# A two-layer graph kernel on one core: in the layer-1 visit stage SyncE runs 4000 empty loop turns ahead of the stage's closing barrier

## What is computed

```python
h = (x @ W).reshape(n, NHEAD, OUT_FEATS)                  # NHEAD 4, OUT_FEATS 64
h_l, h_r = (a_l * h).sum(-1), (a_r * h).sum(-1)
e = h_l[row] + h_r[col]
e = jnp.where(e > 0, e, ALPHA * e)
m = jax.ops.segment_max(e, row, num_segments=n)
ex = jnp.exp(e - m[row])
denom = jax.ops.segment_sum(ex, row, num_segments=n)
msg = (ex / (denom[row] + 1e-16))[:, :, None] * h[col]
out = jax.ops.segment_sum(msg, row, num_segments=n)
```

```python
xn = ln(x)
x = x + L0_gnn(xn, src, dst, edge_weight) + L0_mix(xn)
x = x + L0_ffn(ln(x))
xn = ln(x)
x = x + L1_gnn(xn, src, dst) + L1_mix(xn)
x = x + L1_ffn(ln(x))
```

## Time and profile before

| | |
|---|---|
| time, median of 3 runs | 4206.16 us (4198.36 to 4212.7) |
| span of the profiled execution | 4207.4 us |
| PE, PEld busy | 2730.2 us (65%), 2053.4 us (49%) |
| DVE busy | 2571.9 us (61%) |
| POOL busy | 2199.0 us (52%) |
| ACT busy | 1421.0 us (34%) |
| HBM traffic | 314.12 MB read, 62.05 MB written |

### The profile page before, as it was taken

The page is one execution under the profiler, slowest core; times in us unless marked ns, Lnnn a source line. Parts: engine busy times, 40 slices in busy tenths (PEclk is TensorE's granted clock), DMA queues, the critical chain, the costliest instruction groups (busy, mean ns, idle before and its releaser), DMA issues. The chain is left out here.

```text
span 4207.4 us, 47856 instructions
## 1 busy us (share of the span) xinstructions
PE 2730.2 (65%) x12850; PEld 2053.4 (49%) x12850; DVE 2571.9 (61%) x5963; ACT 1421.0 (34%) x4306; POOL 2199.0 (52%) x2162
## 2 busy tenths in 40 slices
PE   5476777577777653815666666666666655699984
PEld 4243444355555543614544444444444435599972
DVE  5346998677777786435455565556555567544438
ACT  6663000077777731113221111111111113333334
POOL 0466777666666602573256665666665641255530
PEclk9778887788989865957777777777777775699985
DMA  5332333233333223622223333333333354222234
GB/s 145 87 87 82 89 88 87 86 87 93 89 93 95 86 67 87 159 62 66 69 78 86 91 87 85 87 89 89 89 87 86 87 79 159 76 72 70 71 92 145
DMA packets 204009, 379.38 MB, mean 90 GB/s; under 512 B 48926, under 2 KB 131873, under 8 KB 203619
## 3 DMA queue, kind: packets, MB, share of 16 engines
q0 software_dynamic: 102192, 279.12, 24.7%
q1 hardware_dynamic: 101556, 97.19, 7.5%
HBM read 314.12 MB, written 62.05 MB: 89 GB/s over the span
## 5 line engine op out<-in xcount | busy, mean ns | idle before, releaser
L534 POOL DMA_INDIRECT arena<-h_table,arena x1712 | 1729.3, 1010 | 1082.5 <-issue 479.2
L548 DVE TENSOR_TENSOR arena<-arena,ps 128x260 f32 (+1 forms) x1712 | 719.3, 420 | 848.1 <-remote 355.2
L2196 PE MATMUL ps<-arena 128*128 128x260 f32 x1760 | 674.2, 527 | 376.2 <-DVE arena L548 162.2
L1216 PE MATMUL ps<-arena 128*128 128x256 f32 x1664 | 556.6, 451 | 243.4 <-DVE arena L548 133.3
L2196 PEld LDWEIGHTS ps<-arena 128*128 128x128 f32 x1760 | 411.7, 258 | 534.5 <-issue 249.7
L1216 PEld LDWEIGHTS ps<-arena 128*128 128x128 f32 x1664 | 326.6, 221 | 400.1 <-issue 237.5
L717 ACT ACTIVATE arena<-arena 128x112 f16<-128x112 f16 x1568 | 446.7, 375 | 94.5 <-DVE arena L983 77.9
L2045 ACT ACTIVATE ps<-arena 128x32 f32<-128x32 f32 x110 | 22.1, 201 | 1036.9 <-DVE arena L2109 909.5
L884 DVE TENSOR_SCALAR arena<-arena 128x128 f32<-128x128 f32 x832 | 289.5, 349 | 0.4
L2120 DVE TENSOR_TENSOR arena<-arena,ps 128x1024 f32<-128x1024 f32 x220 | 267.1, 1214 | 2.1 <-ACT ps L2045 2.1
L2570 ACT ACTIVATE arena<-ps,arena 128x128 f32<-128x128 f32 x456 | 143.6, 366 | 307.1 <-PE ps L2618 274.6
(11 more groups left out here) (525 smaller groups left out, 4486.5 us busy)
## 6 DMA issues: line engine op xcount, KB each, us to landing
arena<-h_table,arena POOLq DMA_INDIRECT x1712
arena<-in_L_ffn_w SPq DMA_DIRECT2D x32, 512.0 KB, 7.7
xn_table<-arena SPq DMA_DIRECT2D x14, 896.0 KB, 4.0
slot_out<-arena SPq DMA_DIRECT2D x21, 512.0 KB
arena<-y_rows SPq DMA_DIRECT2D x12, 896.0 KB, 9.5
h_table<-arena SPq DMA_DIRECT2D x7, 924.0 KB
h_table<-arena SPq DMA_DIRECT2D x7, 896.0 KB, 4.2
arena<-in_x SPq DMA_DIRECT2D x48, 128.0 KB
```

What stands on the lines that cost most here:

```text
L534: pool.indirect_dma_start(slot[:, 0:width], None, table, bass.IndirectOffsetOnAxis(ap=idx, axis=0)).then_inc(done, 16)
L548: dve.tensor_tensor(to, to, bank(b, width), ALU.add).then_inc(gnn_add, 1)
L1216: pe.matmul(bank(n % V0_BANKS, D), hot_w[:, g % 2, u, :], rows[:, n % RING, :], start=True, stop=True).then_inc(gnn_ps, 1)
L2196: pe.matmul(bank(4 + (g * U + u) % GNN1_BANKS, ACC_W), hot[:, b, u, :], rows[r][:, u, 0:ACC_W], start=True, stop=True).then_inc(gnn_ps, 1)
```

## The change

SP gets a function in the block of the layer-1 visits: a loop of 4000 turns with nothing in it. Nothing is taken away, and no other engine's function is touched. The loop issues no DMA and touches no semaphore; when it is through, SP goes to the block's closing barrier as before.

```diff
@@ -2011,6 +2011,7 @@
         LW = PARTS * 2 * GH
         ZERO_W = 100
+        TURNS = 4000
         assert BUCKETS * ACC_W % ZERO_W == 0
...
@@ -2018,6 +2019,11 @@
         with nc.Block() as block:
+            @block.sync
+            def _(sp):
+                with sp.Fori(0, TURNS):
+                    pass
+
             @block.gpsimd
             def _(pool):
```

## The result

The changed kernel takes 4518.18 us (median of 4 runs, 4509.96 to 4527.73) against 4203.15 us of before beside it (4 runs, 4198.36 to 4212.7): a ratio over the runs of 1.0739, 95% interval 1.0712 to 1.0766 (the two medians alone give 1.075). That is 315 us slower where 4206 us, no change, was forecast.

The account below looks back on a forecast made before the run. The visits on the other four engines, VectorE last at the barrier, were taken to bound the stage; SP's 960 us loop would hide within its 1414.4 us wait. Terms summed to 0, so 4206 us, range 4193 to 4235.

Parts of the forecast that it names:

- What bounds the kernel now: Visits stage: SP waits 1414.4 us at the closing barrier, VectorE comes last, no engine is full.
- the ring: Visits: GpSimd's gathers wait 269.1 us for TensorE, VectorE's additions 211.2 us for TensorE; SP has no part.
- The turn: SP's loop: branch 0.15 plus addition 0.09 makes 0.24 us, bounds 0.15 and 0.40, from neighbouring instructions.
- Does a running SP slow the others?: Visits: the loop adds no DMA, semaphore update or instruction fetch traffic, so it costs the other engines nothing.
- I price contention at nothing: Visits: a running SP's effect on the others put at zero, at most the scatter of the times of before.
- The sum: 4000 x 0.24 = 960 us of loop, SP at the barrier at 3007 us, 454 before VectorE; total change 0.
- The break-even of 0.354 us a turn: Closing barrier: the loop stays hidden while a turn takes less than 1414.2 / 4000 us.
- Rival A: Turn above 0.354 us makes SP last at the barrier; 4232 us at 0.36, 4392 at 0.40; chance 0.10.
- Rival B: Loop straddles an instruction-page step, each turn paying 0.34 us extra: 0.58 us a turn, 5112 us; chance 0.08.
- pushes code across the step: Loop shifts an instruction-page step of 0.34 us from behind the first load to before SP's barrier; gain put at nothing.
- Rival C: Loop isn't executed (4206 us, SP's drain stays at 2047.0), or a gain without known mechanism; first half within the 0.80.
- The range: Whole kernel: 4193 (scatter) to 4235 us (turn of 0.36 us), leaving out most of A, and B, some 0.17.

Follow-up runs that it names:

- turns_2000: Changed kernel with 2000 loop turns instead of 4000: 3658.8 us against 3658.98 of before, ratio 1.0001.
- no_gathers_2: Changed kernel, 4000 turns, GpSimd's gathers from the 33rd visit on replaced by semaphore increments; a repeat: 3747.07 us against 4211.93 of before.
- plain_dma_2: Changed kernel, 4000 turns, indirect gathers from the 33rd visit on replaced by plain DMAs of 128 rows; a repeat: 3729.37 us against 4186.04 of before.
- turns_8000: Changed kernel with 8000 loop turns instead of 4000: 4330.4 us, 671 more than before.
- nops_2: Changed kernel with 4000 written-out no-operations on SP in place of the loop; a repeat: 4219.7 us against 4211.93 of before.
- in_experts_2: Kernel before plus 1500 empty SP turns in the layer-1 expert stage, none among the visits; a repeat: 4177.47 us against 4186.04 of before.
- in_experts: Kernel before plus 1500 empty SP turns in the layer-1 expert stage, none among the visits; first run: 3659.04 us against 3670.7 of before.
- act_turns: Kernel before, no SP loop, 150 empty turns on ScalarE early in the visits; first run: 3660.87 us against 3658.98 of before.

## Why the prediction was wrong

**What bounds the kernel now** held: SP is no part of the ring, and with 2000 turns nothing moved. Of the gathers it said only that GpSimd and TensorE wait for each other. The 283.8 us of "remote" in the earlier trace rows, the largest wait of the group, were passed over. They are VectorE's wait for TensorE's counter `gnn_ps`, whose increments come late. In every trace of the long condition with all its gathers line 548 has such waits, in turns_2000, no_gathers_2 and plain_dma_2 it has none in this stage: a sign of the condition, though not yet of a held SP.

**The turn**, 0.15 + 0.09 = 0.24 us, was right for a turn that nothing disturbs: 0.225 us, 6% less. Its rows were SP's own instructions at the ends of blocks, where no gather is in flight: GpSimd's drains ahead of them are over at 1785.6 and 1978.1 us. That price was used for a stretch in which 880 gathers run. But no row of before shows the hold. Among the visits VectorE's 880 register instructions of line 548 took 69 ns each, part of the earlier trace rows, and TensorE's 880 of line 2177 took 55 ns each. So the trace could not have given the held price; the text could only have named the case. The upper bound of 0.40 us came from an instruction of VectorE and was meant for another kind of instruction, not for company; the mean, 0.430 us, is beyond it all the same.

**"Does a running SP slow the others?"** is the step that failed. Its answer, nothing, is not refuted by the runs: 1404.8 us for the others' work, and 1407.5 us with 2000 turns, but 1420 and 1422 us in two other runs with a loop. The question in the other direction, whether the others slow a running SP, was not put. "I price contention at nothing" was thus applied to both, and it left out 4000 x (0.430 - 0.225) = 820 us. With it the sum is 900 + 820 = 1720 us, against 1404.8 us of cover: 315 us, as measured. The seven tenths of cover that the forecast used up (960 of 1414 us) left room for a turn 1.5 times as dear, and it was 1.8 times.

**The sum** fails with it: SP's drain at 3779.3 instead of 3007. The break-even of 0.354 us a turn and the rule behind it (each us beyond the stage is a us of the kernel) are what the trace shows, and what turns_8000 gives at its own price.

**Rival A** has the right outcome for another reason. By its test (drain last, turn below 0.5 us, queue 14 unchanged) it is A. But its reason was a dear jump, and nops_2 shows the same holds without one. Its chance of 0.10 was drawn for that reason alone.

**Rival B** falls. Queue 14 carries the same 148 packets and 1.21 MB, and the turn is an even 0.225 us as soon as the gathers are over. That the loop pushes code across the step agrees with the trace; the first loads behind the barrier, against the earlier trace rows (start, us, what):

```profile
3779.62 0.39 SPq L2291 DMA_DIRECT2D arena<-in_L_ffn_gate_w  x1
3780.07 0.45 SPq L2293 DMA_DIRECT2D arena<-in_L_ffn_gate_b  x1
3780.57 0.54 SPq L2294 DMA_DIRECT2D arena<-in_L_ffn_b  x1
```

The gap behind the first load is 3780.07 - 3780.01 = 0.06 us where it was 0.39. It seems to stand ahead of the drain now, which starts 0.4 us after the last branch (3778.9, 3779.3) instead of 0.2 (2030.49, 2030.65 at line 1734). **Rival C** falls: the loop is executed.

**The range** ended at 4235, at a turn of 0.36 us. It went only as far as the cases that had a reason; the case that came had none in the text.

**What stays open.** Shown is that, in the long condition, a dense stream of instructions on SP or ScalarE is held while indirect DMAs from GpSimd are in flight. Why is not shown. Three things point the same way: the hold goes about by the instruction and not by its kind, ScalarE's loop is held like SP's, and in the same stretches records of every kind are missing, of landings and of the engines' increments. That would fit a path that all records share and that backs up. Two things speak against it, or at least aren't explained by it: the sparser streams of the other engines show no held instruction (69 and 55 ns, above), and the expert stage has more instruction records per us than the visits (27 in in_experts_2, 14 in the changed kernel) and an eighth of the hold. The Trainium skill, page "NOTIFIC — the notification-queue block", section "Overflow: three behaviours, one of which stalls the engine", describes such a thing: the block's inner pipeline makes its producers wait rather than lose a record. No run here shows that block, and the missing records would need another behaviour that the same section lists, so this is argued only. Nor do the runs say whether an execution that is not recorded would be held: every timed run has a span and a clock on record, the timed runs (4518.18 us) and the profiled one (4527.73) agree, and so all of them have the holds. The 315 us are shown for recorded executions only. What switches the condition was not found either. TensorE's granted clock doesn't: among the visits it is 0.73 in before and 0.83 with 2000 turns in the short condition, but 0.91 and 0.90 with plain DMAs in the short and the long one, so it goes with the stage's course and not with the occasion.

## What to carry to other kernels

A duration from a quiet place, such as a barrier, is a lower bound. Even rows of the same stretch need not show what a new, dense stream will meet there: here they showed no hold, and only a run of the stream in its company gave its price. "What does this do to the others" has to be asked in both directions.

Work on an idle engine is free only up to the time at which the last engine comes to the barrier. Work out the price at which it stops being free and compare it with the forecast; where they are as near as 0.354 and 0.24 us a turn, a bound from another engine's instruction is a thin reason to call the work hidden. Where a large wait has a releaser that the profile can't name, look up which semaphore the instruction waits for in the kernel before giving the wait a cause.

## What the runs showed of the hardware

- Where nothing holds it, an empty loop turn (addition and compare-branch) takes 0.225 us on SP in the visits (turns_8000), 0.251 us at another place in SP's stream (in_experts), and 0.215 us on ScalarE (act_turns). An instruction that does nothing takes 39 ns in a row of 4000, an increment of a semaphore 61 ns.
- In the long condition single instructions of SP or ScalarE are held some 0.7 us at a time, up to 1.4 us as recorded, while indirect DMAs run: 0.14 to 0.16 us an instruction in the mean on SP among 880 gathers in some 1400 us, 0.08 us on ScalarE in the first 57 us of them, 0.02 us on SP among 224 indirect DMAs in 436 us, none among plain DMAs at 134 GB/s.
- The same kernel on the same chip took 3659 or 4212 us on two occasions. Cutting a gather from 260 to 16 words a row leaves the stage at 1423 us; making it a plain DMA brings it to 953 us.
- In the long condition semaphore records go missing while indirect DMAs run: 3,977 of 14,080 landings and 566 of 881 increments of VectorE are on record in the visits of before, 13,729 and 880 with plain DMAs (plain_dma_2).
